# Two running sums instead of four for the adding scatters, and a closing stage that reads two rows per token

## The reference, cut to what matters

```python
topk_w, topk_ids = jax.lax.top_k(scores, TOP_K)               # TOP_K = 8
...
g = jax.lax.ragged_dot(sorted_tokens, jnp.swapaxes(w_gate, 1, 2), group_sizes)
u = jax.lax.ragged_dot(sorted_tokens, jnp.swapaxes(w_up, 1, 2), group_sizes)
h = jax.nn.silu(g) * u
out = jax.lax.ragged_dot(h, jnp.swapaxes(w_down, 1, 2), group_sizes)
unsorted = jnp.zeros_like(out).at[sort_idx].set(out)
y = (unsorted.reshape(B * S, TOP_K, D) * topk_w[..., None]).sum(axis=1)
...
x = _layernorm(x + _L1_ffn_ref(x, ...), axis=-1)              # (x - mean) / sqrt(var + 1e-05)
```

## Time and profile before

| | |
|---|---|
| Median of three runs | 4667.4 us |
| Profiled execution, its own time | 4671.13 us |
| Its span, first to last instruction | 4669.3 us |
| Mean granted TensorE clock | 0.967 of full |
| TensorE busy | 4139.6 us, 89% of the span |
| VectorE busy | 3336.0 us, 71% |
| ScalarE busy | 2754.4 us, 59% |
| GpSimd busy | 2391.4 us, 51% |
| Moved by DMA | 419.03 MB, mean 90 GB/s |

### The profile page before, as it was taken

How to read it: one execution, slowest core, us unless ns; L and a number is a source line. 1 busy time by engine, 2 the same in 40 slices (tenths; PEclk the granted TensorE clock), 3 DMA queues, 4 the chain that set the end, 5 groups by cost and what they waited for, 6 DMA issues and landing times. The chain is left out here.

```text
span 4669.3 us, 80269 instructions
## 1 busy us (share of the span) xinstructions
PE 4139.6 (89%) x18254; PEld 2805.0 (60%) x18255; DVE 3336.0 (71%) x7116; ACT 2754.4 (59%) x6638; POOL 2391.4 (51%) x1811
## 2 busy tenths in 40 slices
PE   7888888779999979999999999999986639999997
PEld 2333333236666547777777777777765527777775
DVE  7999999954343668888888888888866543333335
ACT  6777777622212008888888888888863214444442
POOL 5999899720000014444444545444537766566653
PEclk8999999999999989999999999999998869999999
DMA  2222222220100461122121212122136537777777
GB/s 74 77 77 77 77 91 74 97 87 28 65 31 17 150 192 30 41 58 51 38 51 40 59 37 52 38 53 54 41 93 197 186 110 155 158 157 150 160 150 217
DMA packets 344711, 419.03 MB, mean 90 GB/s; under 512 B 68752, under 2 KB 276240, under 8 KB 339104
## 3 DMA queue, kind: packets, MB, share of 16 engines
q1 hardware_dynamic: 243888, 299.10, 21.4%
q0 software_dynamic: 53760, 73.44, 7.6%
q10 hardware_dynamic: 46944, 45.16, 4.7%
HBM read 251.67 MB, written 165.87 MB: 89 GB/s over the span
## 5 line engine op out<-in xcount | busy, mean ns | idle before, releaser
L1811 DVE TENSOR_TENSOR probsT<-ps_t,probsT 128x512 fp32r<-128x512 f32 (+3 forms) x1280 | 781.1, 610 | 120.0 <-ACT probsT L1744 101.6
L1735 ACT ACTIVATE probs<-ps_s,negm 128x512 f32<-128x512 f32 (+3 forms) x1297 | 814.3, 628 | 42.8 <-DVE negm L1794 39.7
L1584 PE MATMUL ps_o<-probsT,vbuf 128*128 128x512 f32 (+3 forms) x2560 | 823.4, 404 | 13.7 <-DVE probsT L1811 6.6
L1561 PE MATMUL ps_s<-kbuf,qbuf 128*128 (+1 forms) x2602 | 769.1, 382 | 69.9 <-ACT probs L1735 44.4
L1744 ACT ACTIVATE probsT<-ps_t 128x512 fp32r<-128x512 f32 (+3 forms) x1280 | 687.7, 537 | 147.1 <-PE ps_t L1572 118.2
L1572 PE MATMUL ps_t<-idn,probs 128*128 128x128 f32 x4352 | 690.8, 274 | 13.6 <-DVE probsT L1811 13.3
L569 POOL TENSOR_TENSOR dBx<-u,b_all 128x1024 f32<-128x1024 f32 x255 | 610.9, 2411 | 93.3 <-DVE h L666 54.5
L1572 PEld LDWEIGHTS ps_t<-idn,probs 128*128 128x128 f32 x4352 | 528.9, 140 | 161.6 <-DVE probsT L1811 31.6
L2612 POOL DMA_INDIRECT sum<-y,place x288 | 448.4, 1557 | 318.8 <-DVE y L2649 309.3
L1561 PEld LDWEIGHTS ps_s<-kbuf,qbuf 128*128 128x128 f32 x2602 | 446.8, 190 | 227.4 <-ACT probs L1735 101.1
L1783 DVE TENSOR_REDUCE least<-ps_s 128x1 f32<-128x512 f32 x781 | 531.5, 681 | 31.1 <-PE ps_s L1561 30.7
(11 more groups left out here) (270 smaller groups left out, 7081.3 us busy)
## 6 DMA issues: line engine op xcount, KB each, us to landing
room_b<-xs ACTq DMA_DIRECT2D x294, 136.0 KB, 2.6
room_a<-q_scr SPq DMA_DIRECT2D x528, 64.0 KB, 1.9
b_all<-b_scr SPq DMA_DIRECT2D x32, 1024.0 KB, 4.7
room_a<-W_guT SPq DMA_DIRECT2D x64, 384.0 KB, 4.2
q_scr<-rot SPq DMA_DIRECT2D x64, 256.0 KB, 2.7
rspread<-r_scr SPq DMA_DIRECT2D x64, 256.0 KB, 3.4
attn_T<-ostage SPq DMA_DIRECT2D x128, 128.0 KB, 2.2
at<-attn_T SPq DMA_DIRECT2D x32, 512.0 KB
```

What stands on the lines that cost most here:

```text
L1561: last = nc.tensor.matmul(ps_s[:, u % RING, 0:w], qbuf[:, BAND * s + j, :], kbuf[:, bass.ds(kslot, 1), part, c * CW:c * CW + w], start=par ...
L1584: last = nc.tensor.matmul(ps_o[:, lo:], vbuf[:, kb, :, :], probsT[:, g % SLOTS, part, lo:], start=kb == 0 and part == 0, stop=kb == BAND * ...
L1735: nc.scalar.activation(probs[:, k, at:at + n, :], ps_s[:, u % RING, 0:n * P], ACT.Exp, bias=negm[:, tile, :], scale=-1.0, accum_out=sums[: ...
L1811: nc.vector.tensor_tensor(probsT[:, g % SLOTS, 1, lo:], ps_t[:, t % 2, lo:], probsT[:, g % SLOTS, 0, lo:].bitcast(F32), ALU.subtract).then ...
```

## The change: what it does

`SUMS` goes from 4 to 2, and with it:

- `mamba` zeroes one sum after each chunk instead of three: 8 transfers of 512 KB in place of 24.
- In `experts` the scatters alternate between two sums, and scatter g waits for scatter g - 2 instead of g - 4. `y_freed` of a group is now given two groups after its scatter instead of four.
- `combine` loads two parts of each pair, 32 loads of 256 KB instead of 64, into eight slots instead of four, in the same space. The first filling is 16 loads in both. TensorE makes two matmuls per tile, and GpSimd's addition of the parts is gone.

Besides, the inverse deviation is computed on GpSimd in two small instructions per tile (add epsilon, raise to the power -0.5) instead of two on ScalarE and three on VectorE. VectorE's order is written anew.

```diff
--- before.py
+++ after.py
@@ -1856,7 +1856,7 @@
 I32 = mybir.dt.int32
 U32 = mybir.dt.uint32
 EXPERTS, TOPK, FF = 64, 8, 192
-SUMS = 4
+SUMS = 2
 SPARE = 16
 MAXG = TOKENS * TOPK // P + EXPERTS + SPARE
 ROW = DM + 16
@@ -2408,7 +2408,7 @@
     nc.all_engine_barrier()
 
 
-SUM_SLOTS, SUM_TILES = 4, 2
+SUM_SLOTS, SUM_TILES = 8, 2
 
 
 def sum_rows_of(nc, room):
@@ -2683,23 +2683,18 @@
         o_sb = sb("o_sb", [P, SLOTS, DM])
         stats = sb("stats6", [P, RING, 6])
         mv = sb("mv6", [P, RING, 2])
...
         rstd = sb("rstd6", [P, RING, 1])
         eps_sb = sb("eps6", [P, 1])
+        nhalf = sb("nhalf6", [P, 1])
         ps_r = ctx.enter_context(nc.psum_tensor("ps_r6", [P, BANKS, 512], F32))
 
         eps_set = tally("eps_set6")
...
         aggr = tally("aggr6")
...
+        eps_added = tally("eps_added6")
+        powered = tally("powered6")
         o_ready = tally("o_ready6")
         o_out = [tally("o6_out%d" % s, 16) for s in range(SLOTS)]
 
@@ -2719,34 +2714,18 @@
                     pe.wait_ge(in_ld[g % SUM_SLOTS].sem, in_ld[g % SUM_SLOTS].at(g // SUM_SLOTS))
                 if t >= BANKS:
                     pe.wait_ge(o_ready.sem, o_ready.at(t - BANKS))
-                for a in range(SUMS - 1):
-                    if j == 0 and a == SUMS - 2:
-                        pe.wait_ge(added.sem, added.at(g))
+                for a in range(SUMS):
                     last = nc.tensor.matmul(ps_r[:, t % BANKS, 0:DM], idn, parts[:, g % SUM_SLOTS, a, j * DM:(j + 1) * DM],
-                                            start=a == 0, stop=a == SUMS - 2)
+                                            start=a == 0, stop=a == SUMS - 1)
                 last.then_inc(summed.sem, 1)
 
         @block.scalar
         def _(act):
-            def inv_std(t):
-                h = t % RING
-                act.wait_ge(aggr.sem, aggr.at(t))
-                nc.scalar.activation(log[:, h, :], mv[:, h, 1:2], ACT.Ln, bias=eps_sb[:, :]).then_inc(log_done.sem, 1)
-                act.wait_ge(log_done.sem, log_done.at(t))
-                if t >= RING:
-                    act.wait_ge(newton.sem, newton.at(t - RING))
-                nc.scalar.activation(guess[:, h, :], log[:, h, :], ACT.Exp, scale=-0.5).then_inc(guessed.sem, 1)
-
             def store(t):
                 act.wait_ge(o_ready.sem, o_ready.at(t))
                 act.dma_start(out[t * P:(t + 1) * P, :], o_sb[:, t % SLOTS, :]).then_inc(o_out[t % SLOTS].sem, 16)
 
-            nc.scalar.preload_act_table_set("natural_log_exp_and_others")
-            act.wait_ge(eps_set.sem, 1)
-            inv_std(0)
             for t in range(NT):
-                if t + 1 < NT:
-                    inv_std(t + 1)
                 store(t)
             for s in range(SLOTS):
                 act.wait_ge(o_out[s].sem, o_out[s].at(NT // SLOTS - 1))
@@ -2754,11 +2733,20 @@
         @block.gpsimd
         def _(pool):
             nc.gpsimd.memset(eps_sb[:, :], EPS).then_inc(eps_set.sem, 1)
-            for g in range(PAIRS):
-                s = g % SUM_SLOTS
-                pool.wait_ge(in_ld[s].sem, in_ld[s].at(g // SUM_SLOTS))
-                nc.gpsimd.tensor_tensor(parts[:, s, SUMS - 2, :], parts[:, s, SUMS - 2, :], parts[:, s, SUMS - 1, :], ALU.add
-                                        ).then_inc(added.sem, 1)
+            nc.gpsimd.memset(nhalf[:, :], -0.5).then_inc(eps_set.sem, 1)
+
+            def inv_std(t):
+                h = t % RING
+                pool.wait_ge(aggr.sem, aggr.at(t))
+                if t >= RING:
+                    pool.wait_ge(o_ready.sem, o_ready.at(t - RING))
+                nc.gpsimd.tensor_tensor(rstd[:, h, :], mv[:, h, 1:2], eps_sb[:, :], ALU.add).then_inc(eps_added.sem, 1)
+                pool.wait_ge(eps_added.sem, eps_added.at(t))
+                nc.gpsimd.tensor_tensor(rstd[:, h, :], rstd[:, h, :], nhalf[:, :], ALU.pow).then_inc(powered.sem, 1)
+
+            pool.wait_ge(eps_set.sem, 2)
+            for t in range(NT):
+                inv_std(t)
 
         @block.vector
         def _(dve):
@@ -2771,43 +2759,23 @@
                 dve.sem_inc(stat_seen.sem)
                 nc.vector.bn_aggr(mv[:, t % RING, :], stats[:, t % RING, :]).then_inc(aggr.sem, 1)
 
...
             def norm_rows(t):
                 h, s = t % RING, t % SLOTS
-                dve.wait_ge(newton.sem, newton.at(t))
+                dve.wait_ge(powered.sem, powered.at(t))
                 if t >= SLOTS:
                     dve.wait_ge(o_out[s].sem, o_out[s].at(t // SLOTS - 1))
                 nc.vector.tensor_scalar(o_sb[:, s, :], ps_r[:, t % BANKS, 0:DM], mv[:, h, 0:1], rstd[:, h, :], ALU.subtract,
                                         ALU.mult).then_inc(o_ready.sem, 1)
 
-            add_stats(0)
-            moments(0)
-            add_stats(1)
+            for t in range(2):
+                add_stats(t)
+                moments(t)
             for t in range(NT):
-                if t + 1 < NT:
-                    moments(t + 1)
-                norm_square(t)
                 if t + 2 < NT:
                     add_stats(t + 2)
-                norm_part(t)
-                norm_rstd(t)
                 norm_rows(t)
+                if t + 2 < NT:
+                    moments(t + 2)
     nc.clear_and_free_semaphores(sems)
     nc.all_engine_barrier()
 
```

More of the change, by code:

```diff
@@ L2685, in combine @@
         mv = sb("mv6", [P, RING, 2])
[L2686 to L2689, removed]
         rstd = sb("rstd6", [P, RING, 1])
         eps_sb = sb("eps6", [P, 1])
+        nhalf = sb("nhalf6", [P, 1])
         ps_r = ctx.enter_context(nc.psum_tensor("ps_r6", [P, BANKS, 512], F32))
         eps_set = tally("eps_set6")
-        added = tally("added6")
         summed = tally("summed6")
@@ L2699, in combine @@
         aggr = tally("aggr6")
-        log_done = tally("log6_done")
-        guessed = tally("guessed6")
-        newton = tally("newton6", 3)
+        eps_added = tally("eps_added6")
+        powered = tally("powered6")
         o_ready = tally("o_ready6")
```

## The result

The change makes the kernel 0.5% slower: 4695.2 us (median of five runs, 4691.7 to 4700.7) against 4670.9 us, a ratio of 1.0053 with a 95% interval of 1.0042 to 1.0065. The forecast was 4648 us. The closing stage gave what the sum said, 20.9 us against 20.7. The experts stage took 46.6 us longer where the sum had 0.5 us.

A forecast was written before the change was run, and what follows sets the result against it. Bounds: TensorE in experts, VectorE with full DMA engines in combine. Profiled execution: 4671.1 - 20.7 (combine) + 0.5 (experts) = 4650.9 us; on the median 4667.4 - 20.2 = 4647.2, say 4648 us, range 4641 to 4657 us.

The forecast's parts named there:

- Combine, -20.7 us: Closing stage: last norm at 4645.3 instead of 4666.0 us, from 10 tiles at 1.2 us and 21 at 1.0 us.
- The stated range: Combine's gain was put between 11 us (1.3 us per tile) and 24 us (0.9 us per tile).
- The clears, 0: First stage: 16 fewer transfers of 512 KB beside a busy VectorE change nothing, bounded by 1 us each way.
- Experts, +0.5 us: Scatter stage: nearly no loss, since TensorE stays full; lower end nothing, upper end 31 us plus some 5 us.
- the delay stops at 5.4 - 5.2 = 0.2 us and does not add up: Experts: a scatter starting later waits less behind the load of `xr`, so its delay stays 0.2 us.
- 3.8 + 1.0 = 4.8 us per two scatters: Experts: landing plus wake-up of a scatter alone, under the 5.19 us at hand, so delayed scatters catch up.
- The phase argument: Experts: scatters starting later against TensorE's beat meet the `xr` load less; landings of 4.0 or 3.8 us against 4.4.
- landings at 4.2 us or less: Experts: a sign that the forecast is right, alongside scatters still 2.60 us apart.
- Three groups of slots as a cushion: Experts: three groups of slots lie between GpSimd and a stall of VectorE, whose `place` waits eight groups back.
- The rival, +31 to +36 us: Experts: landing plus wake-up, 5.4 us against 5.19 us for two groups, sets the pace; 4680 us total, chance 0.14.
- The round-robin rule: Experts: DMA engines alternate between queues packet by packet, so a later scatter still shares with the load and lands later.
- The lock of the shared ports: Combine: GpSimd and VectorE operations may exclude each other; 0.12 us per pair would cost 4 us of the gain.

The follow-up runs named there:

- The run with small weights: The changed kernel loading only 48 of 384 and 32 of 256 weight columns from the fifth expert on; experts took 745.3 us.

## Why the prediction was wrong, point by point

- **Combine, -20.7 us: right** in size (-20.9), and nearly in its parts: the first norm comes 2.2 us earlier counted from the last scatter (1.9 forecast), the norms take 33.1 us (33), slots of `o_sb` were short while loads ran. Two small errors cancel in the 33.1: the first ten tiles took 13.1 us instead of 12, the other 21 took 19.9 instead of 21. The stated range does not follow from its own terms: 31 x 1.3 and 31 x 0.9 us give gains of 13.4 and 25.8 us, not 11 and 24.
- **The clears, 0: right** as far as the traces show.
- **Experts, +0.5 us: wrong, +46.6.** The step that failed is "the delay stops at 5.4 - 5.2 = 0.2 us and does not add up", with its price for a scatter on its own, "3.8 + 1.0 = 4.8 us per two scatters". The phase argument in it was right as far as it went: scatters out of step with the rows' load land after 4.0 us in the median instead of 4.4. But the weight loads were left out. Before, each comes 1.5 us after a scatter's start and hits it little; once the beat is lost they come at any point, 74 of 288 landings take 5.13 us, and the mean is 4.36 us, hardly less than the 4.42 of before. The run with small weights shows it from the other side: there landings take 4.15 us and the stage loses nothing. And the wake-up was taken as 1.0 us for every scatter; it is 1.01 us in the median but 1.16 in the mean, since 100 scatters start right behind the one before them (less than 1.9 us), held up by GpSimd's own 1.56 us. (4.36 + 1.16) / 2 = 2.76 us per scatter; in the means this holds by definition, and what the traces add is how the 5.52 us are made up. A row of 3.8 us from one scatter in a lull was made the price of all, although a maximum of 5.6 us stood in the earlier trace rows beside it. That scatter was also read wrongly: it started 1.9 us later than the beat (4142.56 against 4138.02 + 2.60), not 2.7. And the sign "landings at 4.2 us or less" came true in the median, 4.0 us, while the stage lost 46.6 us: it should have been the mean.
- **Three groups of slots as a cushion: wrong in kind.** They even out single delays, but here every pair of scatters is late, and TensorE, 99% busy before, has next to no idle time in which to make up what it loses. After the change the slots are full: the 8.5 us for which a `y` waits are about three scatters of 2.76 us. This is read from the rows; no run varied the slots.
- **The rival, +31 to +36 us:** its mechanism is what happened. The price was too low. Its landing of 4.4 us fits the mean, 4.36, though for another reason; its wake-up of 1.0 us was the median, and the mean is 1.16. So the loop came to 5.52 us instead of 5.4, 0.06 us more per scatter, or 17 us over the stage.
- The round-robin rule of the Trainium skill ("DMA: Bandwidth & Descriptors", "Queues, rings and completion order"), by which I had placed this rival, agrees with the landings here in that those beside a burst of another queue are longer, by 1.0 us in the mean; other ways of sharing would show the same, and no run tells them apart. The lock of the shared ports, which the prediction took from the Trainium skill ("SBUF — State Buffer"), did not show: in the closing stage after, each of the 32 adds took 0.19 us.

## What to carry to other kernels

Fewer buffers in flight turn a latency into a rate: price such a change as (landing + wake-up) / number in flight, with the means of both under load and not the medians, and compare it with the beat of the engine that is full. When the two are within a few per cent, each 0.1 us in the loop counts (n / in flight) times; put the wait for the landing last, directly before the instruction that needs it. With the late wait, two sums beat both kernels (0.997 and 0.996 of the kernel before in two sets of runs); three sums with the early wait gave as much (0.997).

## What the runs showed of the hardware

- On GpSimd, a wait for a landing with two more waits, already fulfilled, and one increment between it and the DMA costs 0.24 us more from the signal to the DMA's start than one moved behind them (1.01 against 0.77 us in the median).
- An adding scatter of 128 rows keeps GpSimd 1.56 us, an overwriting one 0.96 us. The adding one moves in 144 packets of 102 ns in the median, the overwriting one in 48 of 171 ns.
- An adding scatter lands after 5.6 us when the load of an expert's weights is issued in its first 1 us, and after 3.8 us when it is issued 1.5 to 3.5 us after its start (means over 36 and 55 scatters of the kernel after).
